# A flash-style attention stage: the order of the two kinds of transposing DMA on SyncE's queue

## The reference

```python
q = (x @ Wq + bq).reshape(Bsz, Tlen, NUM_HEADS, HEAD_DIM)
kv = x @ Wkv + bkv
k, v = (kv[..., :HEAD_DIM], kv[..., HEAD_DIM:])
...
scores = jnp.einsum('bhqd,bkd->bhqk', q, k) * scale
scores = jnp.where(causal[None, None, :, :], scores, jnp.finfo(scores.dtype).min)
probs = jax.nn.softmax(scores, axis=-1)
attn = jnp.einsum('bhqk,bkd->bhqd', probs, v)
...
s = _L0_attn_ref(xn, ...)
g = _silu(_L0_ffn_ref(xn, ...))
x = x + s * g
```

## Time and profile before

| | before |
|---|---|
| median of 3 runs | 1045.0 us (1044.33 to 1047.13) |
| the profiled execution's own time | 1045.0 us |
| its span | 1042.3 us |
| PE busy | 981.1 us (94%) |
| DVE busy | 859.0 us (82%) |
| ACT busy | 638.7 us (61%) |
| POOL busy | 347.4 us (33%) |
| granted TensorE clock | 0.998 |

### The profile page before, as it was taken

One profiled execution on the slowest core, in us unless ns is written; L12 is line 12 of the kernel. 1 busy time (PEld: TensorE's weight loads), 2 busy tenths in 40 slices (PEclk: granted clock), 3 DMA queues, 4 the chain that ended last, 5 costly groups with the idle time before them and its releaser, 6 DMA issues.

```text
span 1042.3 us, 25193 instructions
## 1 busy us (share of the span) xinstructions
PE 981.1 (94%) x8422; PEld 762.9 (73%) x8422; DVE 859.0 (82%) x1697; ACT 638.7 (61%) x1370; POOL 347.4 (33%) x352
## 2 busy tenths in 40 slices
PE   0698999999999999998999999999999999999997
PEld 0566888888889998895666667676776777777776
DVE  6986778778666546558999999999999999999972
ACT  2753333333233333436989889888888888888960
POOL 3205998999897400002101101211112121212111
PEclk9999999999999999999999999999999999999999
DMA  8777678878866522217999999999999999999993
GB/s 283 219 306 182 162 197 182 207 188 191 176 181 159 158 63 68 57 37 187 164 179 194 175 171 173 192 188 178 186 183 186 189 181 177 185 169 166 175 177 97
DMA packets 428269, 179.44 MB, mean 172 GB/s; under 512 B 363850, under 2 KB 417940, under 8 KB 427380
## 3 DMA queue, kind: packets, MB, share of 16 engines
q1 hardware_dynamic: 364272, 131.39, 62.8%
q10 hardware_dynamic: 57396, 28.74, 11.9%
q0 software_dynamic: 6480, 17.70, 7.2%
HBM read 54.94 MB, written 34.87 MB: 86 GB/s over the span
## 4 chain that ended last, share of the span: by engine, by line
PE 38%; DVE 14%; issue 2%; ACT 1%; DMA 0%; DVEq 0%; ACTq 0%
PE b_psS L1347 12%; PE b_psO L1375 11%; PE b_psJ L1392 6%; PE b_psJ L1306 5%; DVE b_ph L1588 5%; DVE b_nmax L1550 4%; PE b_psS L1403 2%; PE b_psO L1378 1%; DVE b_outs L1594 1%; DVE b_psJ L1558 1%; DVE b_Q L1572 1%; DMA b_pT<-b_ph 0%; DVE b_f L1600 0%; DVE b_rrec L1578 0%; ACT b_pr L1457 0%
## 5 line engine op out<-in xcount | busy, mean ns | idle before, releaser
L1007 PE MATMUL psU<-bxT,w_p 128*128 128x256 f16 (+1 forms) x1920 | 287.3, 262 | 5.1 <-DMA bxT<-rowx 3.1
L1098 ACT ACTIVATE h<-psU,bias 128x256 f32<-128x256 f32 (+1 forms) x320 | 124.1, 448 | 249.9 <-PE psU L1007 167.7
L1016 PE MATMUL psY<-w_p,hp 128*128 x1704 | 272.6, 273 | 0.7 <-DVE hp L1128 0.5
L1457 ACT ACTIVATE b_pr<-b_psS,b_nmax 128x1024 f32<-128x1024 f32 (+7 forms) x256 | 188.3, 744 | 54.6 <-DVE b_nmax L1548 36.9
L1347 PE MATMUL b_psS<-b_kp,b_Q 128*128 128x512 f16 (+3 forms) x1152 | 214.9, 326 | 2.5 <-PEq L1187 1.5
L1007 PEld LDWEIGHTS psU<-bxT,w_p 128*128 x1920 | 187.5, 98 | 27.2 <-issue 8.0
L1375 PE MATMUL b_psO<-b_pT,b_vp 128*128 128x256 f16 x1536 | 202.8, 273 | 2.2 <-DVE b_Q L1572 0.9
L1588 DVE SCALAR_TENSOR_TENSOR b_ph<-b_pr,b_rrec,b_ph 128x1024 f16<-128x1024 f32 (+7 forms) x256 | 198.8, 808 | 1.9 <-ACT b_ph L1487 1.9
L1126 DVE CAST hp<-h 128x512 f16<-128x512 f32 (+1 forms) x160 | 92.6, 579 | 118.6 <-ACT h L1098 118.5
L1487 ACT ACTIVATE b_ph<-b_pr,b_rrec 128x1024 f16<-128x1024 f32 (+7 forms) x256 | 188.0, 780 | 0.0
L1016 PEld LDWEIGHTS psY<-w_p,hp 128*128 128x128 f16 x1704 | 165.9, 98 | 22.6 <-issue 2.5
(11 more groups left out here) (195 smaller groups left out, 1069.5 us busy)
## 6 DMA issues: line engine op xcount, KB each, us to landing
wstage<-in_L_ffn_w SPq DMA_DIRECT2D x48, 256.0 KB, 3.4
expert_rows<-rowx SPq DMA_DIRECT2D x67, 128.0 KB, 2.3
expert_outputs<-y ACTq DMA_DIRECT2D x31, 256.0 KB, 2.8
b_pT<-b_ph SPq DMA_TRANSPOSE x320, 3.4
a_x_all<-in_L_attn_x SPq DMA_DIRECT2D x8, 512.0 KB, 9.7
a_w_raw<-in_L_ffn_w SPq DMA_DIRECT2D x4, 1024.0 KB, 9.2
xn_split<-a_xp SPq DMA_DIRECT2D x4, 1024.0 KB, 8.8
xn_turned<-a_xT SPq DMA_DIRECT2D x3, 1024.0 KB, 16.0
```

The lines of the kernel that those rows point to most:

```text
L1007: mm = eng.matmul(psU[w % U][:, g % 2, 0:tiles * P].rearrange("p (t r) -> p t r", t=tiles), weight(n, a * W1 + c * H + g * P, P), bxT[n % ...
L1016: mm = eng.matmul(psY[n % 2][:, t, :], hp[n % 2][:, a, g, t * P:(t + 1) * P], weight(n, 2 * W1 + (2 * g + b) * D, D), start=(g == 0 and k ...
L1098: a = eng.activation(h32[w % 4][:, g, 0:rows], psU[w % U][:, g, 0:rows], ACT.Relu, bias=bias[:, ds(e * HT + 2 * q + g, 1)], scale=1.0 / WS)
L1457: a = eng.activation(pr[k % 3][:, o:o + w], psS[BUF[i]][:, :, :].rearrange("p a n -> p (a n)")[:, o:o + w], ACT.Exp, bias=nmax[:, at:at + ...
```

## The change

In SP's queue, the transpose of a step's low half moves one program step back. Before, program step k issues the high and the low half of step k - 1. Now it issues the high half of step k - 1 and then the low half of step k - 2. In the last program step, in which no high half is left, the last low half is issued alone.

```diff
                 n, i = k // 5, k % 5
                 if 1 <= k <= LAST:
                     turn_hi(k - 1)
-                    turn_lo(k - 1)
+                if k >= 2:
+                    turn_lo(k - 2)
                 if i == 0 and n % HEADS in (5, 6) and n // HEADS + 1 < NH // HEADS:
                     next_v(n // HEADS + 1, n % HEADS - 5)
                 if i == 1 and n >= HEADS + 1:
```

## The result

The changed kernel takes 1073.33 us (median of 4, 1067.65 to 1078.13), the kernel before 1044.66 on the same chip: a ratio of 1.0267, with a 95% interval of 1.0215 to 1.032. A second comparison on another chip gave 1.0172 (1.0123 to 1.0221). So it is slower, as forecast, but by 28.7 us in the first comparison and some 18 in the second, where I had said 11; the first time lies above my range.

A forecast was written before the change was run, and what follows sets the result against it. PE was taken to bound 22 heads, with DVE close behind and bounding heads 2 to 8. The terms 4 + 3.0 + 2.6 + 0 + 1.5 gave 11 us on 1045.0, so 1056 us, range 1044.5 to 1068.

The forecast's parts named there:

- PE's L1375 waits for transposes: Sign in the changed profile: PE's matmuls wait for low halves in many heads between 650 and 900 us.
- 17.3 to 17.7: Sign: time in us that a head takes in the PE-bound stretch after the change, against 17.03 before.
- The rest: Parts 0 to 2 of normal heads and SP's lost time: 0 to 9 us, taken as 1.5.
- step 4: Its low half, needed by part 3 of the values, was held the tightest landing, with 0.2 of 2.7 us left.
- The normal and the tight heads: Heads 9 to 30: 17 normal heads at 0.25 us, 4 us; heads 14, 22, 23 and 29 together 3.0 us.
- The store in head 30: Head 30, past the store: two more issues ahead of a low half PE already awaits; 0.7 to 2.6 us, taken 2.6.
- heads 0 to 8 at 0: DVE-bound early heads, read as 1 to 8: PE's delay is hidden behind DVE, cost 0, otherwise up to 1 us each.
- cover of 1.1 us: Head 7: PE's scores, though delayed, still end 1.1 us before DVE takes them up.
- Sooner landings: Rival: spread transposes land sooner, towards 2.4 us, so margins grow; 1047 or 1045 us; chance 0.22.
- The earlier high halves help: Rival: PE waits for high halves, whose earlier issue gives back up to about 3 us; 1042 us; chance 0.05.
- The DVE stretch breaks: Rival: the cover in the early DVE-bound heads fails, 8 heads add up to 1 us each; 1064 us; chance 0.06.
- SP falls behind: Rival: SP's queue lacks time for its issues, 1 us short in each of 22 heads; 1067 us; chance 0.12.

The follow-up runs named there:

- e10: The kernel before, unchanged, measured once more against itself for a second profile; ratio 1.0023 (0.9993 to 1.0053).
- e6: Against the kernel before, from head 9 on the low halves of steps 0, 1, 3 and 4 moved, step 2 not; ratio 1.0041.
- e5: Against the kernel before, only the low half of step 2 moved behind the next high half, from head 9 on; ratio 1.0085.
- e12: Against the kernel before, only the low half of step 4 moved behind the next high half, from head 9 on; ratio 1.0042.
- e1: Against the kernel before, all low halves moved from head 9 on, old order in heads 0 to 8; ratio 1.0181.
- e2: Against the kernel before, low halves moved only in heads 0 to 8, old order after that; ratio 1.0001.
- e3: Against the kernel before, the changed transpose order with loads, stores and the values' loads also one program step later; ratio 1.0175.

## Why the prediction was wrong

**Right: what bounds, and where the loss would be.** PE bounds heads 9 to 30, DVE follows it, and PE's L1375 waits for transposes. The heads there take 17.0 to 19.0 us where I had said 17.3 to 17.7: the loss sits in some heads and five lose nothing.

**Wrong: "The rest", priced at 1.5 us.** This is the step that failed. I took the median landing of all low halves, 3.3 us, for every step and for the order after the change too, and let margins of 3 us stand against "1.3 to 2.0" us of later issue. In the old order step 2 does land after 3.3 us in the median, with some 3.5 us to spare (e10). But the swap issues it 2.4 us later (in head 12 SP issues it 3.1 us after DVE has ended it, before the change 0.7), and with that beside the gathers, where it lands after 3.8 to 6.0 us. Together that is the whole margin. Nor did part 2 have 3 us: in e10 the low half of step 3 lands some 2.3 us before PE needs it, and in e6 part 2 has 3.0 of the 5.9 us of waits. e5 measures step 2 alone: 6.4 us. With steps 0, 1 and 3 (e6 less e12: 2.3 us, a difference of two single profiles) "the rest" is about 9 us, the very end of the bound that I gave and then didn't use.

**Oversized: step 4.** The normal and the tight heads were 7 us; e12 gives 4.7, with 3.8 of waits. The landing of step 4, with half the columns, takes 2.5 to 2.7 us in the five recorded in e1 and not 3.3, so the normal head keeps a margin near 1 us, and the loss lies in single heads such as 13 and 21 (18.3 and 18.0 us in e12), whose low half is behind the load of values. My sum had no term for that load. In the changed kernel part 3 hardly waits (1.1 us); I take it that PE has already lost the time in part 1. The store in head 30 was to cost 2.6 in part 2; PE waits there in another part, 1.47 us in part 1.

**Wrong: heads 0 to 8 at 0.** I had read head 7, where the cover of 1.1 us does hold. PE waits for low halves in most of these heads (9.3 us together), but DVE, which bounds them, loses time in one place only: from its first low half of head 0 to that of head 5 it takes 81.7 us in the changed kernel and 81.6 before, from there to head 7 36.5 in place of 32.0, and from there to head 9 32.0 in both. I had not read head 4, the one behind whose last step the queue loads values. The changed kernel there:

```profile
567.99 1.32 SPq L1707 DMA_TRANSPOSE b_pT<-b_ph  x1
569.41 1.26 SPq L1712 DMA_TRANSPOSE b_vp<-later_kv  x1
570.77 1.28 SPq L1701 DMA_TRANSPOSE b_pT<-b_ph  x1
...
572.10 2.68 SPq L1707 DMA_TRANSPOSE b_pT<-b_ph  x1
...
578.36 0.80 PE L1375 MATMUL b_psO<-b_pT,b_vp 128*128 128x256 f16 x3 [3.31 <-DMA b_pT<-b_ph]
```

DVE had this low half ready at 569.35. It goes at 572.10, behind the load of values and the next high half, and lands some 6 us later, as PE's wait tells; the landing itself was not recorded (in the second profile of the changed kernel it was, with 4.8 us). PE stands for 3.31 us, more than the cover. And a second loss comes on top, in the columns of the earlier trace rows:

```profile
574.00:577.00 3.00, 1.06 (x11) 0.74 (x8) 3.00 (x7) 3.00 (x8) 0.67 (x1) 1.00 0.75 177
577.00:584.00 7.00, 5.64 (x17) 2.46 (x18) 4.05 (x9) 3.79 (x8) 0.00 (x0) 0.52 1.01 198
584.00:590.00 6.00, 6.00 (x55) 4.59 (x54) 4.79 (x9) 4.62 (x10) 0.00 (x0) 1.00 0.69 130
```

While PE stands, its granted clock falls from 2.4 to 1.2 GHz for 6.8 us, and DVE, the bound in this stretch, is busy for 4.05 of 7 us. The head takes 18.95 us in place of 16.02. In the kernel before there is no such fall in the attention stage until the very end. The second profile of the changed kernel shows one too, at 586.6 us; e2 and e3 show the longer stretch (160.6 and 160.1 us) without it. So the wait is the cause and the clock an addition in some executions: DVE's 32.0 us become 34.6 and 34.1 without the fall, 36.5 and 35.6 with it. In e3, where the load of values comes a step later, it is not head 4 that is long (15.8 us): there PE waits 1.5 us in part 0 of head 5, the first part whose low halves go out behind the load. That this stretch costs 3 to 5 us rests on four profiles; the times of e2 neither show nor exclude it.

**The rivals.** Sooner landings came for step 4 alone: 2.5 to 2.7 us in e1, where e10 has 2.4 to 4.9 with a median of 2.9. "The earlier high halves help" had nothing to give back: in the profile of the kernel before, PE's only wait for a transpose in the attention stage is the 0.68 us of the earlier trace rows, for a low half. "The DVE stretch breaks" came true in part: DVE loses 2 to 4.5 us, around heads 4 and 5 and not by up to 1 us in each of eight heads. "SP falls behind" gave nearly the time, but its mechanism is not there: SP waits more than before, and its DMA queue fills 88.3% in place of 93.0%. The Trainium skill (DMA: Bandwidth & Descriptors, section on the anatomy of one DMA) has a fixed cost of about 2.0 us, fitted on GpSimd's path, and a part that grows with the bytes; it misses here in the direction that matters: 2.4 us was the least from the start of an issue, and 6.0 us stands beside two gathers.

**The sum.** Measured in the attention stage: 6.4 (step 2), 4.7 (step 4), 2.3 (the other steps), 5 (heads 0 to 8), together 18. The forecast had 7 for step 4, 2.6 for head 30, 1.5 for all other steps and 0 for heads 0 to 8, together 11. The other 9 us between the first two profiles are in the expert stage, whose instructions are the same; that they are scatter is likely by the other profiles, and not shown.

## What to carry to other kernels

Read the latency of a transfer by its place in the cycle, not as the median of its line: what runs beside it is the same each time round, so one place is slow, and a reorder can move a transfer into it. A DMA moved back in an in-order queue inherits the waits of what stands in front, and also meets other traffic; add both before comparing with the margin, and look for the rare neighbour (here a load in six heads) as well as for the common one. Margins of 2 to 3 us in front of the bounding engine are spent quickly when a queue is nine tenths full.

## What was not expected of the hardware

- The transpose of 1024 columns lands, from the start of its issue, in the median after 3.2 to 3.3 us at the steps away from the gathers (steps 0, 1 and 2 of e10), and after 4.8 us just behind two gathers of 128 rows of 1 KB (step 3 of e10); in e1, beside the gathers, step 2 took 3.8 to 6.0 us.
- Waits of 3.3 and 2.7 us of TensorE in a stage that is otherwise dense were accompanied by 6.8 and 3.4 us at 1.2 GHz; one of 2.4 us (e2) by none.
- The kernel's own time scattered more on the later chips (1041.8 to 1060.8 us) than on the first (1044.3 to 1047.1 in four runs). As far as the profiles show, the scatter lies in the expert stage: heads 9 to 30 of the unchanged order took 372.8, 372.5, 373.1 and 371.6 us in four profiles, the last two with later gathers.
